# Second attention of a two-layer block rewritten: paired row maxima, probability sums on POOL, keys loaded once per batch, one order over all groups

## What is computed

```python
# H = 16 heads, D = 64, ROPE = 32, NOPE = 32, latent width R = 32
q = concat(q_nope, rope(q_rope));  k = concat(kv, rope(k_rope))
v = concat(kv, zeros)
att = einsum('bhqd,bhkd->bhqk', q, k) / sqrt(64)
att = softmax(where(causal, att, -inf))          # 2048 x 2048 per head and batch
y = einsum('bhqk,bhkd->bhqd', att, v) @ Wo
```

## Time and profile before

| | us |
|---|---|
| median of 3 runs | 3430.34 (3423.89 to 3437.43) |
| the profiled execution | 3437.6 |
| its span (first to last instruction) | 3435.5 |
| second attention in it, from its first transfer (1511.9) to the next stage (2848.3) | 1336.4 |

### The profile page before, as it was taken

One profiled execution on the slowest core, in us unless ns is written; L12 is line 12 of the kernel. 1 busy time (PEld: TensorE's weight loads), 2 busy tenths in 40 slices (PEclk: granted clock), 3 DMA queues, 4 the chain that ended last, 5 costly groups with the idle time before them and its releaser, 6 DMA issues. The chain is left out here.

```text
span 3435.5 us, 49722 instructions
## 1 busy us (share of the span) xinstructions
PE 2976.4 (87%) x19024; PEld 1795.3 (52%) x19024; DVE 2101.8 (61%) x3814; ACT 1577.8 (46%) x3161; POOL 1120.7 (33%) x394
## 2 busy tenths in 40 slices
PE   3768999999999646669999999999999993888788
PEld 2534444454444235545555555555555552766666
DVE  4647777776776046667767667676767632444444
ACT  1224676675666312213555555555555552333332
POOL 3410000000000035523757566566666581111111
PEclk8967999997999568878999999999999996999899
DMA  3670331233020056574231322232322101001100
GB/s 94 193 119 4 42 43 16 34 43 42 11 38 6 26 174 199 173 196 111 51 73 49 73 68 65 57 85 50 80 61 65 35 7 62 31 31 31 62 31 13
DMA packets 168061, 227.33 MB, mean 66 GB/s; under 512 B 51024, under 2 KB 92624, under 8 KB 164880
## 3 DMA queue, kind: packets, MB, share of 16 engines
q1 hardware_dynamic: 166960, 219.17, 26.6%
q10 hardware_dynamic: 864, 4.98, 0.5%
HBM read 141.51 MB, written 81.79 MB: 65 GB/s over the span
## 5 line engine op out<-in xcount | busy, mean ns | idle before, releaser
L1025 ACT ACTIVATE a_prob<-a_pS 128x512 f32<-128x512 f32 (+3 forms) x1280 | 661.8, 534 | 571.8 <-PE a_pS L1144 302.2
L603 DVE TENSOR_REDUCE a_rowmax<-a_pR 128x2 f32<-128x1024 f32 (+3 forms) x640 | 650.8, 1061 | 203.7 <-PE a_pR L642 120.8
L584 ACT ACTIVATE a_prob<-a_pS 128x512 f32<-128x512 f32 (+3 forms) x1280 | 589.1, 538 | 358.9 <-PE a_pS L664 213.4
L998 POOL TENSOR_TENSOR a_zsum<-a_zsum,a_prob 128x2048 f32<-128x2048 f32 (+2 forms) x168 | 695.0, 4137 | 77.2 <-ACT a_prob L1025 62.8
L1144 PE MATMUL a_pS<-a_q,a_key 128*128 128x512 f32 (+7 forms) x2560 | 710.9, 375 | 0.3 <-DMA a_q<-a_neg_lo 0.3
L1048 DVE TENSOR_REDUCE a_rowmax<-a_pR 128x1 f32<-128x512 f32 x768 | 512.9, 687 | 205.6 <-PE a_pR L1122 197.6
L1144 PEld LDWEIGHTS a_pS<-a_q,a_key 128*128 128x128 f32 (+1 forms) x2560 | 451.4, 190 | 105.5 <-ACT a_prob L1025 26.5
L1122 PE MATMUL a_pR<-a_kmax,a_q 128*128 128x512 f32 (+3 forms) x1152 | 443.8, 426 | 2.0 <-DVE a_rowmax L1048 0.7
L664 PE MATMUL a_pS<-a_q,a_key 49*128 49x512 f32 (+3 forms) x1280 | 393.9, 448 | 40.4 <-ACT a_prob L584 31.4
L642 PE MATMUL a_pR<-a_key,a_q 48*128 48x512 f32 (+3 forms) x1280 | 333.7, 459 | 25.8 <-DMA a_q<-mid_qk 16.3
L1052 DVE CUSTOM_DVE_ANT_0 a_pR<-a_pR,causal 128x384 f32<-128x384 f32 (+3 forms) x512 | 250.8, 498 | 155.9 <-PE a_pR L1122 141.2
(11 more groups left out here) (239 smaller groups left out, 4042.8 us busy)
## 6 DMA issues: line engine op xcount, KB each, us to landing
a_q<-mid_q SPq DMA_DIRECT2D x192, 256.0 KB, 6.7
a_key<-mid_k SPq DMA_DIRECT2D x96, 128.0 KB, 3.1
a_key<-mid_qk SPq DMA_DIRECT2D x42, 256.0 KB, 7.9
a_q<-mid_qk SPq DMA_DIRECT2D x42, 256.0 KB, 14.3
mid_qk<-p_qk_hi SPq DMA_DIRECT2D x32, 256.0 KB, 2.9
mid_qk<-p_qk_lo SPq DMA_DIRECT2D x32, 256.0 KB, 3.4
mid_q<-p_n_hi SPq DMA_DIRECT2D x32, 256.0 KB, 3.0
mid_q<-p_n_lo SPq DMA_DIRECT2D x32, 256.0 KB, 3.3
```

Of the source, the lines that this page charges most:

```text
L584: act.activation(prob[:, n % 4, h, at:GT], pS[:, (HG * n + h) % NS, at:GT], ACT.Exp).then_inc(exp_ready, 1)
L603: dve.tensor_reduce(rowmax[:, c % 2, :, j, t, kc], pR[:, bank, :, 0:n], axis=AX.X, op=ALU.max).then_inc(r_read, 1)
L998: pool.tensor_tensor(zsum[:, :, at:GT], zsum[:, :, at:GT], prob[:, kt % 4, :, at:GT], ALU.add).then_inc(z_added, 1)
L1025: act.activation(prob[:, kt % 4, h, at:GT], pS[:, s_bank(c, kt, h), at:GT], ACT.Exp, scale=SCALE).then_inc(exp_ready, 1)
```

## The change

A new function `attention2` replaces `attention(nc, d, m, True)`.

- R is one item for two heads: head 2j on rows 0 to 63, head 2j+1 on rows 64 to 127, high halves only. The odd head's halves are loaded the other way round, so that its high half lies on rows 64 to 127. There are 80 R in a group instead of 160. A bank of `pR` is now a pair of banks, and there are two of them. DVE reduces both heads off the diagonal in one instruction; on it, it still takes one per head.
- W is gone. POOL adds every step into `zsum`, which is double: 37 instructions in a group instead of 24. Z takes a place in `pR`, 32 times in all instead of 24. DVE makes one reciprocal of 512 columns instead of four.
- The maxima are negated in one piece (one DVE instruction and one transfer).
- Keys are loaded once per batch, three transfers of 64 rows x 2048; values are read from `lat` in place, so POOL's copies go. Queries come in 10 transfers per chunk instead of 6.
- The second S matmul has 65 rows instead of 98.
- One list for the whole stage, written out. It comes from the class `Estimate`, which keeps clocks for PE, ACT, DVE and POOL; R may run up to `LEAD` = 44 items ahead.

```diff
-        NS, NR = 3, 3 if second else 4
+        NS, NR = 3, 2
-        by_pool = lambda c, kt: c > 0 and kt % 4 != 3
+        added_kts = lambda c: range(1 if c else 0, 4 * c + 4)
+        class Estimate:
+            MODES = {"S": P, "R": 64, "V": 32, "M": P, "Z": 32}
+            CYCLE, LATENCY, HANDOVER, SWITCH = 1 / 2400, 0.2, 0.1, 0.06
...
+                if step == "R":
...
+                    for half in range(2):
+                        rows = slice(HALF * half, HALF * half + HALF)
+                        mm = pe.matmul(pR[:, bank, half, 0:n], q0[rows, c, 2 * j + half, P * t:P * t + P], key0[b][rows, GT * kc:GT * kc + n],
+                                       start=True, stop=True)
+                    mm.then_inc(r_psum, 1)
...
+                if step == "Z":
+                    pe.wait_ge(z_added, pool_add[g, c, 4 * c + 3] + 1)
+                    for h in range(HG):
+                        mm = pe.matmul(pR[32 * h:32 * h + 32, bank, 0, :], ones[:, :], zsum[:, c % 2, h, :], start=True, stop=True)
...
+                if c == 0 and kt == 0:
+                    pool.tensor_copy(zsum[:, ring], prob[:, step % 4]).then_inc(z_added, 1)
+                elif c and kt == 1:
+                    pool.tensor_tensor(zsum[:, ring], prob[:, (step - 1) % 4], prob[:, step % 4], ALU.add).then_inc(z_added, 1)
+                else:
+                    pool.tensor_tensor(zsum[:, ring, :, at:GT], zsum[:, ring, :, at:GT], prob[:, step % 4, :, at:GT], ALU.add).then_inc(z_added, 1)
...
+                        act.wait_ge(pv_done, n - 3)
+                        act.wait_ge(z_added, freed_by(every_step[n - 4]))
```

More of the change, by code:

```diff
@@ L827, in attention @@
-        first = order(chain_up(rows(0), rows(1), rows(2, (0, 1, 2))), False)
-        side = chain_up(rows(2, (3,)), rows(3), rows(0), rows(1), rows(2, (0, 1, 2)))
-        body0, body = order(side, True), order(side, True, True)
-        of_next = lambda x: x[0] in "RFM" and (x[1] < 2 or x[0] == "R" and x[1] == 2 and x[3] < 3)
-        final = [x for x in body if not of_next(x)]
-        final += [("Z", NGRP - 1)] + [("N", NGRP - 1, n) for n in range(NTILE)] if second else [("O", NGRP - 1)]
-        bank_uses = lambda items: sum(x[0] in "RMOK" for x in items)
@@ L848, in max_count @@
-        def max_count(items, g, c):
-            return c if items is first else 4 * g + (c if c >= 2 else 4 + c)
+        chunk = lambda g, c: NGRP * g + c
+        FILLS = 3
+        KEY, QUERY = 16 * 3, 16 * 10
+        added_kts = lambda c: range(1 if c else 0, 4 * c + 4)
+        pool_steps = [(g, c, kt) for g in range(NG) for c in range(NGRP) for kt in added_kts(c)]
+        pool_add = {step: n for n, step in enumerate(pool_steps)}
+        every_step = [(g, c, kt) for g in range(NG) for c in range(NGRP) for kt in range(4 * c + 4)]
@@ L949, in _ @@
[L949 to L958 removed]
+            for c in range(2):
+                for dst, src in query_loads(0, c):
+                    sp.dma_start(dst.bitcast(FP32), src).then_inc(q_loaded[c], 16)
@@ L963, in _ @@
         def _(pool):
-            fills = [(t[64:P].bitcast(FP32), 0.0) for t in ((key[1],) if second else (kmax, kmax_first, key[0]))]
-            fills += [(ones[:, :], 1.0)] if second else [(val[:, :, :, 16:32], 0.0), (val[:, :, :, 16:17], 1.0)]
-            fills += [(key[-1][96:98].bitcast(FP32), 1.0)]
-            for n, (place, value) in enumerate(fills):
+            fills = [key1[b][ROWS:ROWS + 1].bitcast(FP32) for b in range(B)] + [ones[:, :]]
+            for n, place in enumerate(fills):
@@ L1031, in _ @@
-            run(act, work)
+            load_keys(act, 0)
+            for item in program:
+                step, g, c = item[:3]
+                if step == "S":
+                    _, _, _, kt, h = item
+                    n = score_step(g, c, kt)
+                    at = first_query(c, kt)
+                    if h == 0 and n >= 4:
+                        act.wait_ge(pv_done, n - 3)
+                        act.wait_ge(z_added, freed_by(every_step[n - 4]))
+                    act.wait_ge(s_psum, HG * n + h + 1)
+                    act.activation(prob[:, n % 4, h, at:GT], pS[:, (HG * n + h) % NS, at:GT], ACT.Exp, scale=SCALE).then_inc(exp_ready, 1)
+                if step == "E":
+                    act.wait_ge(pv_done, score_step(g, c, 4 * c + 4))
+                    if chunk(g, c):
+                        act.wait_ge(r_read, bank_use["Z", *before(g, c)] + 1)
+                    act.activation(oT[:, :], pO[:, :], ACT.Copy).then_inc(o_copied, 1)
@@ L1943, in adaln_moe_kernel @@
             with nc.cleanup_on_exit():
[L1944 removed]
+                attention2(nc, d, m)
             with nc.cleanup_on_exit():
```

661 lines of the change are left out of this document (263 added, 398 removed).

## The result

The changed kernel takes 3457.3 us (median of 20 runs, 3440.7 to 3490.2) against 3430.9 for the kernel before (20 runs, 3402.9 to 3460.9): 1.0082 times as long, 95% interval 1.0056 to 1.0109. That is 26 us more, a small loss, where the prediction's likeliest case was 3437, no change; 3457 lies in its range of 3390 to 3485. The profiled execution took 3465.1 us with a span of 3463.3, which is 27.8 over the span before.

The account below looks back on a forecast made before the run. PE's list was taken to bound the second attention. Stage 1336.4 - 11 (PE) + 8 (Z's waits) - 20 (start) + 30 (finish) = 1343, +7; on the 3430.3 median, 3437 us, range 3390 to 3485.

Parts of the forecast that it names:

- Steady groups: Second attention's repeated groups: PE's list sets their time, 157.5 us each, some 2.9 less a group.
- Z's waits: At each group's end Z waits about 1.2 us in PE's list, scores and R behind it: +8 us in all.
- The rival with cheaper shapes: PE's array shape changes between 128 and 64 rows cost 0.10, not 0.20 us: 3392 us; chance 0.15.
- the slower rival: Two pair banks: R finding no bank stops PE's list, 60 to 70 us of waits with POOL's lag, 3470; chance 0.30.
- The ends: Stage's start and finish: first exponential after 42 us in place of 62 (-20), finish net +30.
- the 1260: PE's time for the main stretch, down from 1271 us, all later maxima included: 1234 work and 26 waiting.
- a clock that falls inside the stage, which it does not now: Listed among the signs that would show the prediction wrong; given no size.
- First exponential: Stage start: loads of 17 to 18 us, then maxima, turning and transfer; 42 us in place of 62, -20.
- The end: Stage's finish after the last maxima: POOL outlasts PE, net +30 us, +27 with the group's -2.9.
- POOL's part: Last two chunks: POOL needs 117 us from the first of their scores.
- The 78 of PE: Last two chunks: PE needs 78 us, as no maxima are left for them.
- The 26 us of waiting: PE waiting in the main stretch, said to stand there now and kept in the forecast beside 1234 us of work.

Follow-up runs that it names:

- e9: Changed kernel with each maxima matmul on all 128 rows of the array in place of 64; 3410.7 us, 0.9932 of the kernel before.
- e7: Changed kernel with the sums of 8 of 16 steps in the last group's last chunk added by PE, not POOL; 3434.2 us.
- e5: Changed kernel with extra matmuls in group 0's three pauses and behind maxima pairs and turnings between chunks' scores; 3435.2 us.
- e12: Changed kernel with maxima of chunks 0 to 2 before the first scores, maxima on 128 rows with their cost estimated, 8 last-chunk sums on PE; 3392.2 us.
- e2: Changed kernel with 22, 20 and 18 extra matmuls in group 0's three pauses alone; 3451.3 us.
- e1: Changed kernel with a chunk's sums (Z) allowed only after the next chunk's maxima are turned; 3454.3 us.
- e11: Changed kernel with maxima on 128 rows and their cost estimated, group 0's pauses and thin stretches filled, 8 last-chunk sums on PE; 3387.7 us.
- e6: Changed kernel with maxima of chunks 0 to 2 first, 220 short matmuls during first loads, two long ones behind each pair before scores; 3460.5 us.

## Why the prediction was right or wrong

**Steady groups: right.** PE's list set them, and its prices held. Forecast -2.9 a group, measured -3.9. The difference is as much as the 8 us (1 a group) that the sum has for Z's waits: they did not come, PE is idle for under 0.3 us a group. A lone pair costs 0.40 beside its columns, the figure that the prediction took from rows without any such pair between full matmuls. By the Trainium skill, TensorEngine Tiling (Array Packing), Key Properties, a change of mode drains the array; the trace agrees, with 0.10 ahead, 0.19 in the pair's own slot and 0.11 behind. The maxima saved on PE were paid back in changes of shape; e9 shows it from the other side. The rival with cheaper shapes (a change at 0.10) is out. POOL: 140 us a group for 147. The copy of 2048 elements took 1.89 us for the 1.9 in the sum, but that was luck: no row gave it, and the prediction's own scaling said 2 to 3. DVE 107 for 119.

**The banks: the slower rival's mechanism is out.** In the steady groups PE waits for the banks in bits, its weight loads for DVE's reading 22 us in 60 places over five groups, mostly while a matmul still runs. The kernel was slower all the same, for a reason that no rival held, so this rival's 0.30 and the room that it gave the range held by luck.

**Group 0: the step that failed.** In "The ends" the prediction took the first maxima's 42 us as the whole price of the start ("up to 14 more while DVE catches up") and put all other work into the 1260 at the full clock. In the kernel before the clock was low up to the first exponential and 1.00 from there to the end, and I read the clock as given:

```profile
1525.00:1573.00 48.00, 45.57 (x91) 24.94 (x92) 45.55 (x134) 0.39 (x1) 0.00 (x0) 0.50 0.90 202
```

Two things were missed. In group 0 the order has Z ahead of the next chunk's first scores, where it has it behind three steps or more of them later on, and the prediction priced Z by the later places; in group 0 its reciprocal lies in the chain to the next scores, and with the small transfer that makes three pauses of 4 to 5 us. And the clock fell with each: 16 us of pauses leave 37 of the 53 that the group takes above its share, against 103 us at the low level. (The 37 is what is left over, not measured by itself; at half of the low time lost, as in e7 and e9, the two would come to more than the 53.) The words "a clock that falls inside the stage, which it does not now" stand in the prediction as what would make it wrong, without a price. e5 holds the clock through group 0 with the waits as they are, and the time follows once its extra matmuls are counted; e12 has neither pauses nor falls, and group 0 takes what the others take. e2 and e5 both fill the long pauses; e2 leaves 89 us at the low level and gains nothing, e5 leaves 21 and gains 19.

**The start and the end: right in sign, mis-sized.** First exponential -31.3 for -20: the loads took 17 us as forecast, but only 4 maxima of chunk 1, not DVE's catching up, stood ahead of the scores. The end +15.4 for +27. POOL's part held: 116.1 us for 117 from the last two chunks' first scores on, with ACT waiting up to 3 us at a time for slots that POOL has to free. The 78 of PE against it did not, since "no maxima are left for the last two chunks" is wrong: 28 pairs of maxima still stand there, up to 2776.8, some 18 us at 0.63, and PE is busy for some 98 up to the last exponential. In the kernel before the same stretch, from chunk 2's first exponential to the sums' matmul, took 102.2; it now takes 116.3. e7 confirms the place and gives 15.8 us back.

**The sum.** The prediction's 7 for the stage would have been -22 with the measured start, end and groups; group 0's 53 made it 31. That 3457 lies in the range of 3390 to 3485 is in part luck: 29 us of pieces that came out better stand against the 53. The 26 us of waiting in the 1260 stand in no row either; the earlier trace rows have PE idle for 11.2 us of the 1271.

## What to carry to other kernels

A pause of PE can cost more than its length: here the clock fell with each of three pauses (16 us together) and was at its lower level for 82 us from there on, of which about half was lost. So look at what an order does at its first round, where leads are not built up yet, and let nothing that DVE does for the last chunk stand ahead of what the next one waits for. Read PE's busy share together with the granted clock and the count of instructions. A half-array pair that stands alone among full-array matmuls cost more here (0.63 us) than its two matmuls one after the other on the full array (0.47); two pairs on end cost 0.43 each.

## What the runs showed of the hardware

In group 0 of the changed kernel the clock fell inside pauses of PE of 4 to 5.3 us. It fell behind pauses of 2.2 and 2.3 us in e1, and twice in e2 with no idle time of over 0.9 us; the first time there was only a stretch in which PE was busy for 1.88 of 3 us. It came back after very different times: 3 us in e11, 7, 7 and 24 in e1, 10 three times in e9, 55 in the changed kernel, 41 at the same place of the same code in e7, 102 in e6 in which PE was busy nearly all the time. Nothing in these traces says what sets that time, and it stays open.

It does not explain how far the runs of one kernel spread: e1 spreads from 3431.8 to 3468.1, but the kernel before, whose group 0 has no fall, from 3402.9 to 3460.9.
